# Order of TensorE's work in the first attention layer of a four-layer block, with the pieces of work around its edges

## The chip, the cores and the metric

One Trainium2 chip, one core. The time is that of one execution on the device, in microseconds (us). Five engines run programs of their own and meet at semaphores: TensorE (PE, matrix products), VectorE (DVE), ScalarE (ACT), GpSimdE (POOL) and SyncE (SP, which issues the DMAs here). DMAs move data between HBM and the SBUF; products land in the PSUM's eight banks.

## What is computed

```python
x = x + cross_attn_two_texts(x, ctx)         # layer l0: 20 heads of 8, keys 0..76 "text", 77..511 "ip"
n = layer_norm(x) * g1 + b1;  x = x + attention(n, n)       # layer a1: 20 heads of 64
n = layer_norm(x) * g2 + b2;  x = x + attention(n, ctx)     # layer a2: 20 heads of 64, 512 keys
n = layer_norm(x) * g3 + b3;  x = x + geglu(n @ w1 + b1) @ w2 + b2    # layer ff
```

x is (8, 256, 160), ctx is (8, 512, 256), all float32. In l0, softmax runs over the text keys and the ip keys apart, and the two weighted sums are added. Its projections are q = x Wq, k = text Wk, v = text Wv and the same for ip.

## The kernel before, in words

The eight batches stay in SBUF (`xs`), and the four layers run one after the other, each layer's first steps woven into the last steps of the one before (a seam). Each engine's program is written out by hand, in the order of calls in `build`; no scheduler moves anything, so an instruction that waits holds up all that stand behind it on its engine. Float32 products that must be exact are split into a high and a low part (`hi`, `lo`) in the fp32r type and taken as three products.

**Layer l0** goes in steps t = 0..39 (5 groups of 4 heads for each of 8 batches), a step in four slots s = 0..3. For step t and slot s TensorE's `part(t, s)` (L1689) issues, in this order:
- `score(t, s)` (L1535): scores of group t, into two PSUM banks in turn (`pscore`). For t in 3..34, the middle, a slot with even s issues two of them, s and s + 1, and a slot with odd s none. VectorE's `maximum` (L1867) reduces each to row maxima in two instructions.
- `turned_scores(t-2, s)` (L1550): the same scores with keys on the partitions, into the one bank pair `pst`, which ScalarE's `exp` (L1750) reads; the next one waits for that exponential.
- in slots 0 and 2 half of `weighted_sums(t-3)` (L1638), into `px`.
- in slot 2 `turn_max(t-1)` (L1650): the maxima of the group before are transposed into the bank `pj`; VectorE's `place_max` (L1874) adds them from there to `q4`. On VectorE it is called in slot 2 behind `maximum(t, 2)`.
- in slot 3 of some steps `finish` (L1656, into `px`); then `project(t, s)`, where the plan has something for that slot: a projection of the next batch (L1560, L1567, L1573), the output product (L1662), or a reciprocal's spreading (L1656). All of these but the first values go to `pj`, and each waits until the last user of `pj` has been read.

`EARLY` (L1380) is the plan of the first five steps; `PLAN` that of the others. What is in `FIRST` but not in `EARLY` (`AHEAD`) is projected before step 0.

**The weights of the layers behind** are loaded, copied to `hi` (ACT or POOL) and subtracted to `lo` (POOL) inside the steps of the layer before. For a1 this is `opening(k, s)`, k = t - 24: `WV_HI` (L428) lists the slots in which ACT copies wv's six pieces. The first of them waits for the last stacking DMAs of l0 (`ahead["moved"]`), since it overwrites memory in their reach. POOL rounds each group's stacked keys and queries (`round_stack`, L2005, L2006) and splits each batch's inputs (`split_inputs`, L1971 to L1965).

**Seams.** l0 to a1: for d = 0..2 the four slots of step 40 + d are woven with the two halves of a1's step d. a1 to a2: the context of the first batch is loaded, copied to `hi` by ACT (L1078) and subtracted by POOL (L1281) in a2's `opening(39)`. a2 to ff: VectorE splits w1 and makes the first norm (`xhat`, `n32`) in `opening(k)` behind the last steps of a2.

Of the kernel before, what the change touches and what calls it, by code (L numbers as in the profile page):

```python
# [18 lines left out]
D1 = 64  # L19
INNER = HEADS * D1  # L20
FF = 4 * C
P = 128
# [327 lines left out]
def high_n(act_copy, w, raw_w):  # L350


    act_copy(w[:, 0:2], raw_w[:, 0:2])
    return act_copy(w[:, 4], raw_w[:, 2])


def low_n(subtract, w, raw_w):

    subtract(w[:, 2:4], raw_w[:, 0:2], w[:, 0:2].bitcast(FP32))
    for h in range(2):  # L360
        rows = slice(h * D1 + REST, (h + 1) * D1)
        last = subtract(w[rows, 4], raw_w[rows, 2], w[rows, 4].bitcast(FP32))
    return last


# [16 lines left out]
def self_attention_layer(nc, ctx, places, tag, xs, dram, ln, ahead, next_norm, next_nt):  # L382
# [43 lines left out]


    WV_HI = [(11, 0), (11, 2), (12, 0), (12, 1), (13, 0), (13, 1)]  # L428
# [251 lines left out]
    def vector(dve):  # L680
# [37 lines left out]
        def part(d, i):  # L718
            if here(d - 1):
                if d == 1 and i == 0:  # L720
                    dve.wait_ge(negmax_zeroed, 1)
                maximum(d - 1, i)

        def rest(d):
            if here(d):
                low_queries_keys(d)
# [14 lines left out]
        return dict(opening=opening, part=part, rest=rest)  # L741

    def gpsimd(pool):
# [7 lines left out]
        def opening(k):  # L751
# [36 lines left out]
            if k in (12, 13):  # L788
                pool.wait_ge(wv_hi, 2 * (k - 12) + 2)
                low(wv, k - 12).then_inc(wv_done, 1)  # L790
            if k == 14:
                pool.wait_ge(wv_hi, 6)
                low_rows(wv, wv_done)
                ln.pool_lo(pool, 0, nts[0])
# [17 lines left out]
def cross_attention_layer(nc, ctx, places, tag, xs, dram, ctx_t, ln, nt, ahead, load_next):  # L812
# [42 lines left out]
    ctx_in, c_hi, c_ready = sem("ctx_in"), sem("c_hi"), sem("c_ready")  # L855
# [220 lines left out]
    def scalar(act):  # L1076
# [32 lines left out]
        def opening(d):  # L1109


            if d == 26:
                act.wait_ge(loaded[0], 16)
                high_n(copy, wq, raws["wq"]).then_inc(w_hi, 1)
# [10 lines left out]
            if d == 39:  # L1125
                for s in range(4):
                    high_context(0, s)
# [26 lines left out]
    def vector(dve):  # L1154
        def subtract(out, x, y):
            return nc.vector.tensor_tensor(out, x, y, ALU.subtract)  # L1156

        def low_context(m, s):
            dve.wait_ge(c_hi, 4 * m + s + 1)
# [46 lines left out]
        def opening(d):  # L1206

            if d == 27:
                dve.wait_ge(w_hi, 1)
# [4 lines left out]
            if d == 38:  # L1214
                nc.vector.memset(ones[:], 1.0).then_inc(ones_set, 1)

        def part(d, s):
# [9 lines left out]
            if s == 1 and norm_at(d, LN_STATS):  # L1227
# [7 lines left out]
            if s == 3 and here(d):  # L1235
                low_keys(d)

# [8 lines left out]
    def gpsimd(pool):  # L1246
# [12 lines left out]
        def opening(d):  # L1259
# [6 lines left out]
            if 29 <= d < 33:  # L1266
                s = d - 29
                pool.wait_ge(w_hi, 2)
                nc.gpsimd.tensor_tensor(wk[1][:, s], raws["wk"][:, s], wk[0][:, s].bitcast(FP32),
                                        ALU.subtract).then_inc(wk_done, 1)  # L1270
            if 34 <= d < 38:
                s, cols = (d - 34) // 2, slice((d % 2) * (INNER // 2), (d % 2 + 1) * (INNER // 2))
                pool.wait_ge(w_hi, 3)
# [4 lines left out]
            if d == 39:  # L1278
                for s in range(4):
                    pool.wait_ge(c_hi, s + 1)  # L1280
# [24 lines left out]
def narrow_attention_layer(nc, ctx, places, tag, xs, ident, dram, x_t, ctx_t, load_first, first_in, next_norm):  # L1305
# [67 lines left out]
    def here(g):  # L1373
# [26 lines left out]
    def in_pj(use):  # L1400
        what, m = use
        return not (what[0] == "v" and m < 2)
# [118 lines left out]
    def tensor(pe):  # L1521
# [104 lines left out]
        def weighted_sums(g, half):  # L1626

            m, u = divmod(g, GROUPS)
            if half == 0:
# [3 lines left out]
                if m > 1:  # L1633
# [6 lines left out]
            if half == 1:  # L1640
                last.then_inc(px_ready, 1)

# [46 lines left out]
        def part(t, s):  # L1689


            if here(t) and not V_LAG <= t < ALL - GROUPS:
                score(t, s)
            elif here(t) and s % 2 == 0:
                score(t, s)
                score(t, s + 1)
            if here(t - T_LAG):
                turned_scores(t - T_LAG, s)
            if s in (0, 2) and here(t - V_LAG):
                weighted_sums(t - V_LAG, s // 2)  # L1700
            if s == 2 and here(t - 1):
# [3 lines left out]
            if projected(t, s):  # L1705
                project(*projected(t, s))

# [823 lines left out]
```

## Time and profile before

| | us |
|---|---|
| median of 3 runs | 1583.85 (1581.68 to 1603.56) |
| the profiled execution | 1598.35 |
| its span, first to last instruction | 1596.6 |
| TensorE's mean granted clock in it | 0.968 |
| TensorE busy in it | 1512.6 (95%) |
| VectorE busy | 1082.2 (68%) |
| ScalarE busy | 773.1 (48%) |
| GpSimdE busy | 439.1 (28%) |

The profile is of one execution, 14.5 us above the median. Engine rows give start, duration, engine, line, operation, output and inputs, count; in brackets the idle time before and what ended it. Ends of matmuls are modelled. [...]

### The profile page before, as it was taken

To read this page: it belongs to the slowest core of one execution; us is meant where nothing else is said; L and a number is where in the kernel's file an instruction comes from. 1 tells how busy PE (TensorE), PEld (TensorE's weight loads), DVE (VectorE), ACT (ScalarE), POOL (GpSimd) and SP (SyncE) were. 2 spreads that over 40 slices of the span, in tenths; PEclk is the share of its full clock that TensorE was granted. 3 is DMA by queue.
4 is the path that set the end of the run, shared out by engine and by line. 5 is a ranking of instruction groups with operands and counts; after the bars stand their busy time and mean duration, and the time that the engine had idled before them with its cause. 6 is when DMAs were issued, how large, how long until landed. Compare 5 with 4: busy or idle time off the path is not lost.

```text
span 1596.6 us, 40717 instructions
## 1 busy us (share of the span) xinstructions
PE 1512.6 (95%) x17888; PEld 1190.1 (75%) x17888; DVE 1082.2 (68%) x1515; ACT 773.1 (48%) x1061; POOL 439.1 (28%) x395
## 2 busy tenths in 40 slices
PE   7999999888999999999899999999999999999988
PEld 6556665546888887888678888788888888787788
DVE  5677777662767777767566677676766677676666
ACT  3666666654444455555344444444444454443423
POOL 3333335340222322433321222122211222121300
PEclk7799999977999999999999999999999999999999
DMA  5322222300000020000210010101000020000000
GB/s 153 92 59 59 59 79 69 92 2 2 23 2 2 8 86 2 6 2 4 52 48 2 2 28 1 28 2 28 2 22 7 2 71 2 2 2 1 2 13 21
DMA packets 27211, 45.51 MB, mean 29 GB/s; under 512 B 7392, under 2 KB 15520, under 8 KB 26656
## 3 DMA queue, kind: packets, MB, share of 16 engines
q1 hardware_dynamic: 27040, 42.96, 9.1%
q8 instruction: 140, 2.29, 0.6%
q14 instruction: 31, 0.25, 0.0%
HBM read 29.51 MB, written 1.31 MB: 19 GB/s over the span
## 4 chain that ended last, share of the span: by engine, by line
PE 71%; ACT 8%; DVE 8%; issue 6%; POOL 3%; SPq 2%; DMA 1%; ACTq 0%; POOLq 0%; DVEq 0%
PE a_pj L999 7%; PE a_pj L987 6%; PE a_pj L528 4%; PE a_pv L1021 4%; PE a_px L1021 4%; PE a_px L569 3%; PE l_px L1638 3%; PE a_pv L555 2%; PE a_px L1036 2%; PE l_pst L1550 2%; ACT l_probs L1750 2%; PE a_pscore L931 2%; PE a_pst L952 2%; PE a_px L555 2%; PE a_pj L537 2%
## 5 line engine op out<-in xcount | busy, mean ns | idle before, releaser
L1256 POOL TENSOR_TENSOR a_key_sum<-a_probs 128x512 f32<-128x512 f32 x120 | 159.1, 1330 | 471.7 <-ACT a_probs L1089 471.7
L1168 DVE TENSOR_REDUCE a_negmax<-a_pscore 128x2 f32<-128x1024 f32 x160 | 195.6, 1223 | 106.7 <-PE a_pscore L931 106.3
L1089 ACT ACTIVATE a_probs<-a_pst 128x1024 f32<-128x1024 f32 x160 | 164.0, 1025 | 167.7 <-PE a_pst L958 167.1
L1867 DVE TENSOR_REDUCE l_negmax<-l_pscore 128x2 f32<-128x154 f32 x320 | 201.2, 682 | 55.9 <-PE l_pscore L1535 55.9
L1750 ACT ACTIVATE l_probs<-l_pst 128x1024 f32<-128x1024 f32 x160 | 163.9, 1025 | 90.0 <-PE l_pst L1550 89.7
L748 POOL TENSOR_TENSOR a_key_sum<-a_probs 128x1024 f32<-128x1024 f32 x40 | 96.3, 2407 | 239.0 <-ACT a_probs L617 239.0
L689 DVE TENSOR_REDUCE a_negmax<-a_pscore 128x4 f32<-128x1024 f32 x80 | 97.7, 1221 | 45.9 <-PE a_pscore L486 45.8
L999 PE MATMUL a_pj<-a_wv_hi,a_ct 128*128 128x256 f32 x640 | 112.5, 288 | 0.8
L1193 DVE RECIPROCAL a_recip<-a_pv 128x256 f32<-128x256 f32 x40 | 70.2, 1756 | 45.8 <-PE a_pv L1027 45.8
L617 ACT ACTIVATE a_probs<-a_pst 128x1024 f32<-128x1024 f32 x80 | 81.8, 1023 | 38.9 <-PE a_pst L512 38.1
L1550 PE MATMUL l_pst<-l_q,l_k 32*128 32x256 f32 x640 | 80.2, 330 | 19.7 <-ACT l_probs L1750 19.2
L952 PE MATMUL a_pst<-a_qh,a_kh 64*128 64x256 f32 x640 | 96.1, 293 | 2.7 <-ACT a_probs L1089 1.8
L701 DVE RECIPROCAL a_recip<-a_pv 128x256 f32<-128x256 f32 x40 | 70.3, 1757 | 41.4 <-PE a_pv L560 40.9
L987 PE MATMUL a_pj<-a_ct,a_wk_hi 64*128 64x512 f32 x640 | 94.2, 412 | 2.5 <-POOL a_ct L1281 1.4
L1550 PEld LDWEIGHTS l_pst<-l_q,l_k 32*128 32x128 f32 x640 | 57.2, 202 | 51.4 <-ACT l_probs L1750 43.6
L1638 PE MATMUL l_px<-l_probs,l_v 128*32 128x256 f32 x1280 | 95.2, 419 | 0.0
L954 PE MATMUL a_pst<-a_qh,a_kl 64*128 64x256 f32 x640 | 91.5, 279 | 0.0
L999 PEld LDWEIGHTS a_pj<-a_wv_hi,a_ct 128*128 128x128 f32 x640 | 89.7, 189 | 2.4 <-DVE a_kl L1156 2.3
L958 PE MATMUL a_pst<-a_neg_t,a_sel 64*128 64x256 f32 x640 | 91.1, 277 | 0.0
L956 PE MATMUL a_pst<-a_ql,a_kh 64*128 64x256 f32 x640 | 90.9, 276 | 0.0
L1078 ACT ACTIVATE a_neg_t<-a_pscore 128x256 fp32r<-128x256 f32 x40 | 15.4, 384 | 148.5 <-PE a_pscore L1044 148.5
L1078 ACT ACTIVATE a_v<-a_pj 128x1024 f32<-128x1024 f32 x40 | 41.1, 1027 | 94.0 <-PE a_pj L999 94.0
(239 smaller groups left out, 3654.4 us busy)
## 6 DMA issues: line engine op xcount, KB each, us to landing
l_ct<-in_ctx_t SPq DMA_DIRECT2D x8, 512.0 KB, 3.7
l_k_stack<-l_k_hi SPq DMA_DIRECT2D x64, 64.0 KB, 2.1
a_ct<-in_ctx_t SPq DMA_DIRECT2D x8, 512.0 KB, 4.8
a_ct<-in_ctx_t SPq DMA_DIRECT2D x16, 256.0 KB, 5.6
l_q_stack<-l_q_hi SPq DMA_DIRECT2D x80, 32.0 KB, 1.9
a_raw_wv<-in_a_wv SPq DMA_DIRECT2D x2, 1280.0 KB, 8.4
l_x<-in_x_t SPq DMA_DIRECT2D x8, 256.0 KB, 3.9
l_k_stack<-l_k_lo SPq DMA_DIRECT2D x32, 64.0 KB, 2.1
```

Source lines behind the costliest of these rows:

```text
L689: nc.vector.tensor_reduce(to, pscore[:].rearrange("p h (q k) -> p h q k", q=QT), AX.X, ALU.max, negate=True).then_inc(max_done, 1)
L952: mm(pst[:, h, to], kh[OWN[h], kb, i, kt], qh[OWN[h], qb, i, :], start=True, stop=False)
L987: last = mm(pj[:, t, :], wk[hw][OWN[t], s, u * P:(u + 1) * P], cts[b % 2][OWN[t], hc, s, :], start=k == 0, stop=k == len(C_ROWS) - 1)
L999: last = mm(pj[:, kt // 2, (kt % 2) * STEP_COLS:(kt % 2 + 1) * STEP_COLS], cts[b % 2][:, hc, 2 * s, kt * P:(kt + 1) * P], wv[hw][:, s, u * ...
L1021: mm((pv, px)[x][t * 32:(t + 1) * 32, 0:SQ], v[:, e % 2, kt, t * D1 + x * 32:t * D1 + (x + 1) * 32], probs[:, t, kt, :], start=kt == 0, st ...
L1089: nc.scalar.activation(probs[:, 2 * i:2 * i + 2, 2 * n:2 * n + 2, :], pst[:].rearrange("p h (k q) -> p h k q", k=2), ACT.Exp, scale=SCALE) ...
L1168: nc.vector.tensor_reduce(to, pscore[:], AX.X, ALU.max, negate=True).then_inc(max_done, 1)
L1256: nc.gpsimd.tensor_tensor(key_sums[n][:, two], probs[:, two, 2 * n, :], probs[:, two, 2 * n + 1, :], ALU.add).then_inc(half_summed, 1)
L1550: last = mm(pst[:, h, i * SQ:(i + 1) * SQ], k4[rows, u, kt * P:(kt + 1) * P], q4[rows, u, :], start=True, stop=True)
L1638: last = mm(px[j * ROWS:(j + 1) * ROWS, 0:SQ], vs[m % 2][:, kt, GROUP * u + j, :], probs[g % 2][:, j, kt, :], start=kt == 0, stop=kt == KT ...
L1750: nc.scalar.activation(probs[g % 2][:, 2 * pair:2 * pair + 2, 2 * n:2 * n + 2, :], pst[:].rearrange("p h (k q) -> p h k q", k=2), ACT.Exp, ...
L1867: last = nc.vector.tensor_reduce(to[:, :, k], pscores[s % 2][:, :, keys], AX.X, ALU.max, negate=True)
```

## The change

1. *SBUF addresses* of nearly all tensors (`AT`) are laid out anew.
2. *First steps*: `EARLY` is another plan. The values v1 and v2 of batch 0 are projected ahead of step 0, those of batch 1 come in steps 0, 1, 3 and 4, no longer all in steps 1 and 2.
3. *Middle of l0*: a pair of scores is issued behind the slot's turned scores and weighted sums, no longer ahead of them.
4. *Unread products*: in odd slots of steps 3 to 39 in which nothing is projected or finished, `fill` issues four products of 128x256 that nobody reads.
5. *Weights' pieces*: ACT's six pieces of wv move to later slots; POOL's subtractions for wq and wk are spread over two steps; a2's wq copy is two instructions in two steps.
6. *Seam l0 to a1*: a1's second half step of d = 1 comes ahead of l0's slots 2 and 3 there, and VectorE splits the first queries and keys of a1 between l0's slots 2 and 3.
7. *Seam a1 to a2*: half of the first context is copied and subtracted by VectorE; `maximum` of slot 1 of a2's step 2 comes ahead of a1's normalisation.
8. *Seam a2 to ff*: VectorE's pieces for ff come in slot 1 of their step, with the norm ahead of the split of w1.

```diff
-    WV_HI = [(11, 0), (11, 2), (12, 0), (12, 1), (13, 0), (13, 1)]
+    WV_HI = [(12, 0), (12, 1), (12, 3), (13, 0), (13, 1), (13, 3)]
...
@@ l0, TensorE and the plan
-    EARLY = {(0, 0): ("v1", 0), (0, 1): ("v2", 0), (0, 2): ("ip", 1), (0, 3): ("v3", 0),
-             (1, 0): ("text", 1), (1, 1): ("v0", 1), (1, 2): ("v1", 1), (1, 3): ("v2", 1),
-             (2, 0): ("v3", 1), (2, 1): ("q", 1), (2, 3): ("rest", 1)}
+    EARLY = {(0, 0): ("v3", 0), (0, 1): ("ip", 1), (0, 2): ("v0", 1), (1, 0): ("v1", 1), (1, 1): ("text", 1),
+             (2, 1): ("q", 1), (2, 3): ("rest", 1), (3, 1): ("v2", 1), (4, 1): ("v3", 1)}
...
+        def fill(t, s):
+            if s == 1:
+                pe.wait_ge(pj_read, pj_uses["turn", t - 1])
+            else:
+                pe.wait_ge(px_read, px_uses["sum", t - V_LAG] + 1)
+            k = k4[:, (t - 1) % GROUPS]
+            for _ in range(4):
+                mm((pj if s == 1 else px)[:, 0:SQ], k[:, 0:P], k[:, 0:SQ], start=True, stop=True)
...
-            if here(t) and not V_LAG <= t < ALL - GROUPS:
+            middle = V_LAG <= t < ALL - GROUPS
+            if here(t) and not middle:
                 score(t, s)
-            elif here(t) and s % 2 == 0:
-                score(t, s)
-                score(t, s + 1)
             if here(t - T_LAG):
                 turned_scores(t - T_LAG, s)
             if s in (0, 2) and here(t - V_LAG):
                 weighted_sums(t - V_LAG, s // 2)
+            if middle and s % 2 == 0:
+                score(t, s)
+                score(t, s + 1)
             if s == 2 and here(t - 1):
                 turn_max(t - 1)
             if s == 3 and finished(t):
                 finish(*finished(t))
             if projected(t, s):
                 project(*projected(t, s))
+            elif s % 2 and V_LAG <= t < ALL and not (s == 3 and finished(t)):
+                fill(t, s)
...
@@ a1, POOL's opening
-                if k == first + 2:
+                if k == first + 1:
                     for s in range(2):
                         low(w, s).then_inc(done, 1)
+                if k == first + 2:
+                    pool.wait_ge(*ahead["rounded_in"](OPENED + k))
                     low_rows(w, done)
...
@@ a2, VectorE's opening
+            if d == 39:
+                dve.wait_ge(ctx_in, 48)
+                for s in range(2):
+                    nc.vector.tensor_copy(cts[0][:, 0, s], ct32[:, s]).then_inc(c_first, 1)
+                for s in range(2):
+                    dve.wait_ge(c_first, s + 1)
+                    low_first(s)
...
@@ build, TensorE (ACT the same; DVE with split_first in (0, 1))
             for d in range(3):
                 for i in range(2):
+                    if (d, i) == (1, 1):
+                        own["part"](d, i)
                     first["part"](S0 + d, 2 * i)
+                    if (d, i) == (0, 1):
+                        own["split_first"]()
                     first["part"](S0 + d, 2 * i + 1)
-                    own["part"](d, i)
+                    if (d, i) != (1, 1):
+                        own["part"](d, i)
...
@@ build, VectorE, a1 to a2 and a2 to ff
             cross["part"](2, 0)
+            cross["part"](2, 1)
             own["rest"](S1 + 2)
-            for s in range(1, 4):
+            for s in range(2, 4):
                 cross["part"](2, s)
...
                 for s in range(4):
                     cross["part"](d, s)
+                    if s == 1 and FF_OPEN <= d:
+                        last["opening"](d - FF_OPEN)
                 cross["rest"](d)
-                if FF_OPEN <= d:
-                    last["opening"](d - FF_OPEN)
+                if d == FF_OPEN + 2:
+                    last["scale_first"]()
```

## Rows read from the trace of the kernel before

**Rows 1.** The page: granted clock of TensorE in 40 slices of the span, in tenths

```profile
PEclk7799999977999999999999999999999999999999
```

**Rows 2.** Six stretches of l0: length, busy time of PE, PEld, DVE, ACT, POOL, clock, DMA

```profile
20.50:51.20 30.70, 30.67 (x124) 22.00 (x126) 16.20 (x27) 10.80 (x21) 6.81 (x11) 0.50 0.48 143
80.00:85.00 5.00, 3.96 (x39) 2.14 (x39) 3.94 (x7) 3.55 (x5) 2.17 (x3) 1.00 0.01 2
85.00:90.00 5.00, 5.00 (x32) 3.03 (x30) 1.91 (x4) 2.43 (x3) 0.00 (x0) 0.54 0.06 15
121.60:161.50 39.90, 38.01 (x371) 24.71 (x370) 30.34 (x50) 26.73 (x38) 14.76 (x20) 1.00 0.21 59
269.70:273.10 3.40, 3.40 (x21) 2.01 (x23) 0.87 (x2) 1.40 (x3) 2.75 (x7) 0.50 0.17 42
314.00:337.90 23.90, 19.01 (x116) 10.21 (x116) 9.60 (x16) 13.04 (x18) 4.90 (x7) 0.50 0.02 6
```

**Rows 3.** Timeline of TensorE: slots 2 and 3 of one middle step

```profile
133.95 0.50 PE L1535 MATMUL l_pscore<-l_k,l_q 32*128 32x512 f32 x4
134.31 0.50 PE L1550 MATMUL l_pst<-l_q,l_k 32*128 32x256 f32 x4
134.75 1.07 PE L1638 MATMUL l_px<-l_probs,l_v 128*32 128x256 f32 x16
135.75 0.44 PE L1650 MATMUL l_pj<-identity,l_negmax 128*128 128x128 f32 x2
136.11 0.50 PE L1550 MATMUL l_pst<-l_q,l_k 32*128 32x256 f32 x4
136.70 0.90 PE L1573 MATMUL l_pj<-l_wc,l_ct 128*128 128x160 f32 x6
137.53 0.86 PE L1535 MATMUL l_pscore<-l_k,l_q 32*128 32x512 f32 x4
```

**Rows 4.** Timelines of VectorE and ScalarE in the same two slots

```profile
134.50 1.29 DVE L1867 TENSOR_REDUCE l_negmax<-l_pscore 128x2 f32<-128x154 f32 x2 [0.63 <-PE l_pscore L1535]
136.22 0.42 DVE L1874 TENSOR_TENSOR l_q<-l_q,l_pj 128x256 fp32r<-128x256 f32 x1 [0.44 <-PE l_pj L1650]
...
133.24 1.02 ACT L1750 ACTIVATE l_probs<-l_pst 128x1024 f32<-128x1024 f32 x1 [0.60 <-PE l_pst L1550]
134.86 1.02 ACT L1750 ACTIVATE l_probs<-l_pst 128x1024 f32<-128x1024 f32 x1 [0.38 <-PE l_pst L1550]
```

**Rows 5.** Timeline of TensorE: two starts of steps, five steps apart, and a 256-column projection

```profile
121.58 0.50 PE L1535 MATMUL l_pscore<-l_k,l_q 32*128 32x512 f32 x4
...
155.74 1.24 PE L1560 MATMUL l_pj<-l_nt,l_wq 128*128 128x256 f32 x8
...
161.52 0.50 PE L1535 MATMUL l_pscore<-l_k,l_q 32*128 32x512 f32 x4
```

**Rows 6.** Timeline of TensorE: last work ahead of step 0, its start, start of step 3

```profile
15.54 1.75 PE L1573 MATMUL l_pscore<-l_wc,l_ct 128*128 128x320 f32 x6
18.86 0.50 PE L1535 MATMUL l_pscore<-l_k,l_q 32*128 32x512 f32 x2 [1.56 <-DVE l_q L1942]
...
49.10 0.80 PE L1535 MATMUL l_pscore<-l_k,l_q 32*128 32x512 f32 x4
```

**Rows 7.** Timelines of TensorE and ScalarE: step 35, and the start of step 40

```profile
308.42 0.42 PE L1550 MATMUL l_pst<-l_q,l_k 32*128 32x256 f32 x4
317.77 0.79 PE L1550 MATMUL l_pst<-l_q,l_k 32*128 32x256 f32 x4 [6.24 <-ACT l_probs L1750]
...
362.46 0.79 PE L1550 MATMUL l_pst<-l_q,l_k 32*128 32x256 f32 x4
...
316.07 0.74 ACT L611 ACTIVATE a_wv_hi<-a_raw_wv 128x640 fp32r<-128x640 f32 x1 [6.11 <-DMA l_q_stack<-l_q_lo]
```

**Rows 8.** Timelines: a stall of TensorE in step 30 and one at a seam

```profile
269.07 2.39 PE L1567 MATMUL l_pj<-l_ct,l_wc 128*128 128x512 f32 x6 [1.49 <-POOL l_nt L1965]
...
804.78 0.49 PE L931 MATMUL a_pscore<-a_kh,a_qh 64*128 64x512 f32 x2 [1.92 <-DVE a_negmax L1168]
```

More of the change, by code:

```diff
@@ L40 @@
 AT = {
[24 rows of a table removed]
[19 rows of a table added]
+    210944, "ff_hidden": 5152, "ff_gains": 48672, "a2_ct32": 184160, "ff_ln_half": 48704, "a1_ln_shift": 86336,
[4 rows of a table added]
 }
@@ L347 @@
 STEP_COLS = 2 * P
[L350 to L363, printed above, removed]
 class SplitMatrix:
@@ L425, in self_attention_layer @@
     y_ready, y_taken = sem("y_ready"), sem("y_taken")
-    WV_HI = [(11, 0), (11, 2), (12, 0), (12, 1), (13, 0), (13, 1)]
+    OPENED = ahead["steps"] - 16
+    WV_HI = [(12, 0), (12, 1), (12, 3), (13, 0), (13, 1), (13, 3)]
     WV_HALF = dram["wv"].shape[2] // 2
@@ L722, in part, with split_first @@
                 maximum(d - 1, i)
+        def split_first():
+            low_queries_keys(0)
         def rest(d):
-            if here(d):
+            if here(d) and d > 0:
                 low_queries_keys(d)
@@ L739, in rest @@
                 normalise(d - 3)
-        return dict(opening=opening, part=part, rest=rest)
+        return dict(opening=opening, part=part, rest=rest, split_first=split_first)
     def gpsimd(pool):
@@ L787, in opening @@
                 nc.gpsimd.memset(ones[:], 1.0).then_inc(ones_set, 1)
-            if k in (12, 13):
-                pool.wait_ge(wv_hi, 2 * (k - 12) + 2)
-                low(wv, k - 12).then_inc(wv_done, 1)
+            if k == 12:
+                pool.wait_ge(wv_hi, 2)
+                low(wv, 0).then_inc(wv_done, 1)
+            if k == 13:
+                pool.wait_ge(wv_hi, 4)
+                low(wv, 1).then_inc(wv_done, 1)
+                ln.pool_lo(pool, 0, nts[0])
             if k == 14:
                 pool.wait_ge(wv_hi, 6)
+                pool.wait_ge(ln.n_ready, 1)
                 low_rows(wv, wv_done)
-                ln.pool_lo(pool, 0, nts[0])
         def step(d):
@@ L1113, in opening @@
                 act.wait_ge(loaded[0], 16)
-                high_n(copy, wq, raws["wq"]).then_inc(w_hi, 1)
+                copy(wq[:, 0:2], raws["wq"][:, 0:2]).then_inc(w_hi, 1)
+            if d == 27:
+                copy(wq[:, 4], raws["wq"][:, 2]).then_inc(w_hi, 1)
             if d == 28:
@@ L1125, in opening @@
             if d == 39:
-                for s in range(4):
+                for s in (2, 3):
                     high_context(0, s)
@@ L1156, in subtract, with low_first @@
             return nc.vector.tensor_tensor(out, x, y, ALU.subtract)
+        def low_first(s):
+            subtract(cts[0][:, 1, s], ct32[:, s], cts[0][:, 0, s].bitcast(FP32)).then_inc(c_ready, 1)
         def low_context(m, s):
-            dve.wait_ge(c_hi, 4 * m + s + 1)
+            dve.wait_ge(c_hi, 4 * m + s - 1)
             subtract(cts[m % 2][:, 1, s], ct32[:, s], cts[m % 2][:, 0, s].bitcast(FP32)).then_inc(c_ready, 1)
@@ L1208, in opening @@
             if d == 27:
-                dve.wait_ge(w_hi, 1)
+                dve.wait_ge(w_hi, 2)
                 for h in range(2):
@@ L1226, in part @@
                     ln.dve_lo(dve, norm_at(d, LN_SPLIT), nt)
-            if s == 1 and norm_at(d, LN_STATS):
+            if s == 1 and d > 1 and norm_at(d, LN_STATS):
                 ln.dve_stats(dve, norm_at(d, LN_STATS))
@@ L1236, in part @@
                 low_keys(d)
+            if (d, s) == (1, 3):
+                ln.dve_stats(dve, norm_at(d, LN_STATS))
         def rest(d):
@@ L1267, in opening @@
                 s = d - 29
-                pool.wait_ge(w_hi, 2)
+                pool.wait_ge(w_hi, 3)
                 nc.gpsimd.tensor_tensor(wk[1][:, s], raws["wk"][:, s], wk[0][:, s].bitcast(FP32),
@@ L1278, in opening @@
             if d == 39:
-                for s in range(4):
-                    pool.wait_ge(c_hi, s + 1)
+                for s in (2, 3):
+                    pool.wait_ge(c_hi, s - 1)
                     nc.gpsimd.tensor_tensor(cts[0][:, 1, s], ct32[:, s], cts[0][:, 0, s].bitcast(FP32),
@@ L1401, in in_pj @@
         what, m = use
-        return not (what[0] == "v" and m < 2)
+        return not (what == "v3" and m == 0 or what in ("v0", "v1") and m == 1)
     def finished(t):
@@ L1632, in weighted_sums @@
                     pe.wait_ge(first_read, 4)
-                if m > 1:
+                if m > 0:
                     pe.wait_ge(pj_read, pj_uses["v3", m] + 1)
@@ L2165, in opening @@
             if k == 1:
+                dve.wait_ge(small_in, 64)
+                ln.dve_xhat(dve, 0)
+            if k == 2:
                 dve.wait_ge(w_hi, 1)
@@ L2168, in opening @@
                                         ALU.subtract).then_inc(w_done, 1)
-                dve.wait_ge(small_in, 64)
-                ln.dve_xhat(dve, 0)
-            if k == 2:
+            if k == 3:
                 dve.wait_ge(w_hi, 2)
@@ L2180, in opening, with scale_first @@
                 ln.dve_xhat(dve, 1)
+        def scale_first():
+            ln.dve_n32(dve, 0)
         def batch(b):
@@ L2197, in batch @@
                                     ALU.add).then_inc(y_taken, 1)
-        return dict(opening=opening, batch=batch)
+        return dict(opening=opening, scale_first=scale_first, batch=batch)
     def gpsimd(pool):
@@ L2334, in _ @@
                 for i in range(2):
+                    if (d, i) == (1, 1):
+                        own["part"](d, i)
                     first["part"](S0 + d, 2 * i)
                     first["part"](S0 + d, 2 * i + 1)
-                    own["part"](d, i)
+                    if (d, i) != (1, 1):
+                        own["part"](d, i)
                 own["rest"](d)
@@ L2371, in _ @@
                 for i in range(2):
+                    if (d, i) == (1, 1):
+                        own["part"](d, i)
                     first["part"](S0 + d, 2 * i)
+                    if (d, i) == (0, 1):
+                        own["split_first"]()
                     first["part"](S0 + d, 2 * i + 1)
-                    own["part"](d, i)
+                    if (d, i) != (1, 1):
+                        own["part"](d, i)
                 own["rest"](d)
```

7 lines of the change are left out of this document (3 added, 4 removed), and 47 rows, old and new, of the table AT.

## The prediction

> **What bounds the kernel now.** I read the page's slices first. TensorE's clock falls short of full in the first two slices and again in slices 9 and 10, which are l0's start and its end [rows 1]. Then I took stretches of l0. In the middle TensorE is busy for 38.01 of 39.90 us at full clock; in 20.5 to 51.2 it is busy all the time, at half clock [rows 2]. So a step of the middle can lose little idle time, while the edges hold idle time and half-clock time. The timelines tell which wait ends last at each place.
>
> One middle step shows the structure [rows 3, 4]. Turned scores of two slots can't follow each other in less than about 1.62 us: the exponentials start at 133.24 and 134.86, and each takes 1.02 and a hand-over each way. Slot 2 goes: scores 133.95, turned scores 134.31, weighted sums 134.75, turned maxima 135.75, next turned scores 136.11, projection 136.70. VectorE starts its maximum 0.55 us behind the scores (134.50), finishes it, waits 0.44 for the transposed maxima and places them at 136.22. The projection at 136.70 starts 0.48 us behind that: it writes `pj`, which `place_max` reads. This hand-over, not TensorE's own work, already sets that start.
>
> **The middle of l0 (part 3).** Durations by starts: turned scores 0.33 to 0.43, weighted sums 1.00, scores 0.36, transposes 0.36. In slots 0 and 1 the move is a small gain: the scores fill time in which the next turned scores wait for the exponential, and slot 1 is shorter by 0.34 where it is longer than 1.62. In slots 2 and 3 it is a loss. From the slot's turned scores on, the scores now start at about 1.33 us instead of 0.36 before them. VectorE's maximum starts at 1.33 + 0.55 = 1.88 and ends 1.29 later, at 3.17. `place_max` is called behind it and the projection starts 0.48 behind `place_max`: 3.65. Before, it was 136.70 - 134.31 = 2.39. The projection of slot 3 is late by 1.26 us, and behind it on TensorE stand the next step's turned scores and everything else. TensorE had 0.15 us to spare there; now it stands idle for about 1.2 us.
>
> VectorE can't help itself: `place_max` stands behind a maximum whose scores come late. [...]
>
> The five kinds of step, from [rows 3 to 5] and the plan: slots 2 and 3 take 3.65 us plus the projection (0.8 to 1.7 us), so the five together take about 23.7 us instead of 19.9; slots 0 and 1 take about 19.3 instead of 20.04, after ACT's copies of the last projection, which now stand ahead of the first exponential, have taken back half of the gain. That is +3.8 - 0.8 = +3.0 us on the 39.94 between the two starts of [rows 5]. Five such rounds (t = 10 to 34) give **+15**. Bounds: if the wait is hidden, the 0.34 saved per odd slot remains, -7.5; if the delay of slot 1 adds to it, +20.
>
> **First steps (part 2).** TensorE idles for 1.56 us ahead of step 0 [rows 6]; v1 and v2 fit into that. Steps 0 to 2 take 49.10 - 18.86 = 30.2 us, at half clock, with TensorE dense. The new plan takes four of eleven products out of them (v1, v2 of batch 0 to the front, v2, v3 of batch 1 to steps 3 and 4). Such a product takes 0.83 at full clock (136.70 to 137.53, [rows 3]), up to twice that at half, say 1.5 us: -6, of which VectorE's pace may give 1.5 back, so at least -4.5. [...] I take **-12**, bounds -4.5 and -14. Steps 3 to 9 lose 0.5 to 1 in the ordinary steps and gain where a half-clock stretch such as that from 85 on [rows 2] goes: **-2** (-5 to +2).
>
> **Unread products (part 4).** Eight slots: (3,3), (4,3), (7,1), (36,1), (37,3), (38,1), (38,3), (39,1). A 256-column product takes 1.24 / 8 = 0.15 us, four 0.6, all eight slots 4.9 us if exposed. They stand in slots that wait for the exponential, so I cost them at nothing; without that cover, +4.9. Their worth is the clock, and it is in the terms here.
>
> **Weights' pieces (part 5).** ACT's first piece of wv waits 6.11 us for a stacking DMA in step 35, and the exponential behind it holds TensorE for 6.24; then 23.9 us pass at half clock [rows 7, 2]. One step later (the new slot) is 7 us later, past the DMA's landing at 316. From 308.42 to the start of step 40 at 362.46 are 54.0 us for five steps; at full clock and without the stall they take about 7.1 each (four slots of 1.62 make 6.5, and slot 2 is longer) and 2 more for one output product, 37.5. I take **-14**, bounds -6 (the stall alone) and -17. The POOL pieces were late into step 30 and stalled the projection 1.49 us [rows 8], and 3.4 us at half clock follow it [rows 2]; POOL's wide subtractions now come a step sooner, while it waits for stacking DMAs: **-3**, bounds 0 and -3.5.
>
> **Seams (parts 6 to 8).** TensorE waits 1.92 us for a maximum at 804.78, the pattern of four such stalls of 1.6 to 1.9 us for VectorE [rows 8]: one at the seam to a1, this one, and two at the seam to ff. Each gets the work it waits for moved ahead. With one more wait at the first seam, and with the clock's falls next to the first two: **-4, -4 and -3**. VectorE's share of the first context puts some 2.2 us in front of a maximum of a1, which costs TensorE about what it saves it. Bounds of the three together: 0 and -14. Addresses (part 1): nothing.
>
> **The clock in the middle.** An idle 1.15 us in three of five steps may let the clock fall. [...] I allow two falls at 3 us: **+6**, bounds 0 and +25.
>
> **The sum**, against the profiled execution: 1598.35 - 12 - 2 + 15 - 14 - 3 - 4 - 4 - 3 + 6 = 1577.4. The median stands 14.5 below that execution, and half-clock stretches that come and go are the likely reason; the change takes most of these away in any run, so little of the 14.5 is to be had twice. I take 3.4 off for it: **1574**.
>
> **The rivals.**
> - *The clock falls often in the middle.* One fall in every fourth of 32 steps, at 3 us, is +24, in place of the +6: 1592; one in every second step is +48: 1616. From about five falls on the change is no gain over 1583.85. For it: the stretch at 80 to 85. [...] 0.20, at 1594.
> - *The middle costs nothing.* Place and projection find cover that I don't see, and the exponentials' earlier start counts: -15 from the sum, and no falls (-6), 1553 to 1560. Against it: the projection's start hangs on `place_max` already now [rows 3, 4]. 0.13, at 1557.
> - *The edges give less*, since undisturbed runs do not have the half clock that the profile shows: the start -5 and the last steps -7 instead of -12 and -14, so +14: 1588. For it: the 14.5 us between median and profile. 0.17.
> - *My forecast*: 0.50, own range 1564 to 1584.
>
> **How the numbers follow.** 1574 is the forecast. Up to 0.2 may be left out: the range goes from 1556 to 1600. Within 2% is 1552.2 to 1615.5, about what a measurement of this kernel can tell from no change. Faster needs the second rival at its far end: 0.05. Slower needs a fall in every second step: 0.05. The same: 0.90.
>
> **What would show it.** The step's row of `l_pj` in slot 3 should carry an idle time of 1.0 to 1.3 us put down to VectorE's L1874, in steps without `finish`, and five steps of the middle should take 43 us instead of 39.94. No wait for `l_q_stack` should stand before `a_wv_hi`, and step 3 should start near 37. If five steps take 38 to 40 us, the middle is wrong; if the middle's clock isn't 1.00, the first rival holds. I am wrong in sign if the middle costs over 25 us.

## The result, and the profile after

| | before | after |
|---|---|---|
| median of 20 runs each, us | 1592.66 (1580.38 to 1603.56) | 1598.84 (1593.11 to 1603.13) |
| span of the profiled execution, us | 1596.6 | 1595.5 |
| TensorE's mean granted clock in it (1.00 is full clock, 0.50 half) | 0.968 | 0.979 |

The ratio after to before is 1.0045, 95% interval 1.0023 to 1.0067: the change costs 0.4%, surely more than nothing and well within 2%. The forecast was 1574, the range 1556 to 1600: the result lies just inside the range, 24.8 us above the forecast, and on the other side of the kernel before (a gain of 10 us was forecast, against 1583.85). The three runs of before that the forecast knew (1583.85) lay low; over twenty, before stands 8.8 us higher, and its profiled execution only 5.7 above the median.

The page of the kernel after, granted clock in 40 slices. The low slices of [rows 1] at 9 and 10 are gone; slices 5 and 7, in the middle of l0, are a little lower than before:

```profile
PEclk8999898999999999999999999999999999999899
```

Stretches of l0 in the kernel after, in the columns of [rows 2]. They are: a half-clock stretch in the first steps; five steps of the middle; two half-clock stretches in the middle; the last steps.

```profile
27.10:40.80 13.70, 13.08 (x49) 8.29 (x51) 9.17 (x16) 5.67 (x9) 4.38 (x6) 0.50 0.54 155
120.90:164.22 43.32, 39.04 (x371) 24.38 (x370) 30.27 (x50) 26.71 (x38) 14.79 (x20) 1.00 0.20 55
177.20:190.80 13.60, 13.23 (x83) 7.21 (x84) 7.57 (x11) 5.88 (x8) 6.68 (x9) 0.50 0.22 55
269.20:286.20 17.00, 16.63 (x98) 9.43 (x88) 9.65 (x15) 6.67 (x8) 7.79 (x12) 0.50 0.17 43
323.40:369.50 46.10, 44.33 (x437) 27.52 (x433) 34.68 (x56) 33.00 (x43) 18.47 (x15) 1.00 0.05 12
```

Five steps take 43.32 us at full clock with the same 371 records of TensorE as the 39.90 us of [rows 2]; the engine is busy for 39.04 of them and was for 38.01. The first steps have less than half of the half-clock time of [rows 2] (13.7 us of 30.7), and the last ones none.

Timelines of the kernel after, TensorE and then VectorE, in slots 2 and 3 of one middle step (they answer [rows 3, 4]; here the turned scores are L1558, scores L1543, weighted sums L1646, turned maxima L1670, `maximum` L1891, `place_max` L1898):

```profile
128.99 0.50 PE L1558 MATMUL l_pst<-l_q,l_k 32*128 32x256 f32 x4 [0.29 <-ACT l_probs L1774]
129.42 1.07 PE L1646 MATMUL l_px<-l_probs,l_v 128*32 128x256 f32 x16
130.42 0.51 PE L1543 MATMUL l_pscore<-l_k,l_q 32*128 32x512 f32 x4
130.86 0.44 PE L1670 MATMUL l_pj<-identity,l_negmax 128*128 128x128 f32 x2
131.22 0.51 PE L1558 MATMUL l_pst<-l_q,l_k 32*128 32x256 f32 x4
132.62 0.90 PE L1581 MATMUL l_pj<-l_wc,l_ct 128*128 128x160 f32 x6 [0.89 <-DVE l_q L1898]
...
130.95 1.29 DVE L1891 TENSOR_REDUCE l_negmax<-l_pscore 128x2 f32<-128x154 f32 x2 [0.80 <-PE l_pscore L1543]
132.16 0.41 DVE L1898 TENSOR_TENSOR l_q<-l_q,l_pj 128x256 fp32r<-128x256 f32 x1
132.49 1.29 DVE L1891 TENSOR_REDUCE l_negmax<-l_pscore 128x2 f32<-128x154 f32 x2
```

The chain is the forecast's: scores 1.43 us behind the slot's turned scores, the maximum 0.53 behind them, `place_max` 1.21 later, the projection 0.46 later, 3.63 us in all, where [rows 3] had 2.39. The turned maxima stood ready since 131.3; VectorE comes to them at 132.16 because its maximum is in front.

The other end of the kernel, the seam a2 to ff. TensorE, VectorE and GpSimdE in the kernel after:

```profile
1496.06 0.80 PE L925 MATMUL a_pscore<-a_kh,a_qh 64*128 64x512 f32 x2 [6.28 <-DVE a_negmax L1167]
...
1492.88 0.36 DVE L167 TENSOR_SCALAR ff_ln_xhat<-xs,ff_ln_mv,ff_ln_rstd 128x160 f32<-128x160 f32 x1 [5.60 <-POOL ff_ln_rstd L160]
...
1494.78 1.22 DVE L1167 TENSOR_REDUCE a_negmax<-a_pscore 128x2 f32<-128x1024 f32 x1
...
1486.33 1.29 POOL L1264 TENSOR_TENSOR a_key_sum<-a_probs 128x512 f32<-128x512 f32 x1 [11.20 <-ACT a_probs L1083]
1488.60 1.28 POOL L1264 TENSOR_TENSOR a_key_sum<-a_probs 128x512 f32<-128x512 f32 x1 [0.98 <-ACT a_probs L1083]
1490.92 1.26 POOL L1264 TENSOR_TENSOR a_key_sum<-a_probs 128x512 f32<-128x512 f32 x1 [1.05 <-ACT a_probs L1083]
1492.14 0.70 POOL L160 TENSOR_TENSOR ff_ln_rstd<-ff_ln_var,ff_ln_half 128x2 f32<-128x2 f32 x1
```

VectorE's second normalisation for ff (L167) now stands in slot 1, and the `rstd` that it reads stands on GpSimdE behind three key sums of the same step, each of which waits for one of ScalarE's exponentials. VectorE waits 5.60 us; the maximum behind it comes late, and TensorE stands for 6.28. In the kernel before, the normalisation came behind the whole step (at 1507.74, without a wait), and `rstd` was there since 1501.9.

**Where the time went.** The two traces cut at the same points of the program: `g` is the group whose maxima are turned, `a` a count of the reciprocals in a1 and a2. (`g4`: the maxima of group 4 are turned, in step 5; the seam a1 to a2 is a37 to a40; ff is taken from VectorE's first `ff_hidden` to its last, and some 5 us of either span lie behind it.) With the old order and no fall of the clock, `both_undone` has 37.1 us from g4 to g9 and `mid_undone` 191.9 from g9 to g33.

| stretch | before | after | difference | forecast |
|---|---|---|---|---|
| start to g4 | 71.3 | 61.2 | -10.1 | -12 |
| g4 to g9 (steps 5 to 10) | 39.7 | 42.5 | +2.8 | -2 |
| g9 to g33 | 195.1 | 219.6 | +24.5 | +15 +6 -3 |
| g33 to g39 | 64.5 | 46.1 | -18.4 | -14 |
| g39 to a1's first | 46.3 | 41.6 | -4.6 | -4 |
| seam a1 to a2 | 42.6 | 38.6 | -4.0 | -4 |
| the rest of a1 and a2 | 1030.0 | 1030.9 | +0.9 | 0 |
| last steps of a2 (a77 to ff) | 39.0 | 46.9 | +7.8 | -3 |
| ff | 62.9 | 62.9 | 0 | 0 |
| sum | | | -1.1 | -21 |

### The profile page after: what moved, and what is told of

It reads as the page before. It is cut to its first block, busy times and chain, and to the rows that moved or that the text cites. A ratio compares the mean times of both kernels' runs of the same rounds, so it can differ in the third digit from the quotient of the medians.

```text
span 1595.5 us, 40782 instructions
## 1 busy us (share of the span) xinstructions
PE 1511.8 (95%) x17920; PEld 1183.7 (74%) x17920; DVE 1085.4 (68%) x1519; ACT 772.1 (48%) x1059; POOL 439.9 (28%) x393
## 4 chain that ended last, share of the span: by engine, by line
PE 74%; DVE 10%; ACT 7%; issue 6%; POOL 2%; DMA 1%; SPq 0%; POOLq 0%; ACTq 0%; DVEq 0%
PE a_pj L993 7%; PE a_pj L981 5%; PE l_px L1646 5%; PE a_pj L514 4%; PE a_pv L1015 4%; PE a_px L1015 4%; PE l_pst L1558 3%; PE a_px L555 3%; DVE l_negmax L1891 3%; PE l_pscore L1543 3%; PE a_px L1030 2%; PE a_pv L541 2%; PE a_pscore L925 2%; PE a_pst L946 2%; PE a_px L541 2%
## 5 line engine op out<-in xcount | busy, mean ns | idle before, releaser
L1891 DVE TENSOR_REDUCE l_negmax<-l_pscore 128x2 f32<-128x154 f32 x320 | 202.6, 686 | 95.2 <-PE l_pscore L1543 94.4
L1646 PE MATMUL l_px<-l_probs,l_v 128*32 128x256 f32 x1280 | 91.3, 405 | 2.5 <-DVE l_ot L1911 2.5
L1558 PE MATMUL l_pst<-l_q,l_k 32*128 32x256 f32 x640 | 80.6, 330 | 8.3 <-ACT l_probs L1774 7.8
L1072 ACT ACTIVATE a_v<-a_pj 128x1024 f32<-128x1024 f32 x40 | 41.1, 1027 | 94.2 <-PE a_pj L993 94.2
L1015 PE MATMUL a_pv<-a_probs,a_v 128*32 128x256 f32 x1280 | 85.5, 385 | 0.0
```

The costliest lines, as they stand in the source:

```text
L1015: mm((pv, px)[x][t * 32:(t + 1) * 32, 0:SQ], v[:, e % 2, kt, t * D1 + x * 32:t * D1 + (x + 1) * 32], probs[:, t, kt, :], start=kt == 0, st ...
L1558: last = mm(pst[:, h, i * SQ:(i + 1) * SQ], k4[rows, u, kt * P:(kt + 1) * P], q4[rows, u, :], start=True, stop=True)
L1646: last = mm(px[j * ROWS:(j + 1) * ROWS, 0:SQ], vs[m % 2][:, kt, GROUP * u + j, :], probs[g % 2][:, j, kt, :], start=kt == 0, stop=kt == KT ...
L1891: last = nc.vector.tensor_reduce(to[:, :, k], pscores[s % 2][:, :, keys], AX.X, ALU.max, negate=True)
```

## The experiments

All times are medians; the ratio is to the kernel before, run beside it on the same chip, with its 95% interval. Seven of the variants have only four runs, so differences of medians and of ratios can part by several us; where they do, both are given. "From" names the kernel that was edited.

| run | from | us | ratio |
|---|---|---|---|
| `mid_alone` | before | 1634.71 | 1.0302 (1.0238 to 1.0367) |
| `mid_undone` | after | 1564.51 | 0.9839 (0.9781 to 0.9898) |
| `place_first` | after | 1575.83 | 0.9903 (0.9871 to 0.9935) |
| `norm_back` | after | 1594.52 | 1.0005 (0.9975 to 1.0035) |
| `both_undone` | mid_undone, norm_back | 1556.41 | 0.9744 (0.9667 to 0.9820) |
| `rstd_first` | mid_undone | 1558.31 | 0.9758 (0.9679 to 0.9837) |
| `take_first` | place_first, norm_back | 1560.37 | 0.9767 (0.9690 to 0.9844) |
| `no_fill` | mid_undone | 1567.97 | 0.9799 (0.9722 to 0.9877) |
| `old_first` | mid_undone | 1573.68 | 0.9853 (0.9776 to 0.9929) |
| `old_wv` | mid_undone | 1579.77 | 0.9931 (0.9902 to 0.9961) |
| `wv_alone` | before | 1580.32 | 0.9918 (0.9874 to 0.9962) |
| `fill_wait` | norm_back | 1576.40 | 0.9893 (0.9829 to 0.9958) |

**1. The order of the middle alone, and everything but it.** `mid_alone` puts it into the kernel before, `mid_undone` takes it out of the kernel after:

```diff
-            middle = V_LAG <= t < ALL - GROUPS
-            if here(t) and not middle:
+            if here(t) and not V_LAG <= t < ALL - GROUPS:
                 score(t, s)
+            elif here(t) and s % 2 == 0:
+                score(t, s)
+                score(t, s + 1)
...
-            if middle and s % 2 == 0:
-                score(t, s)
-                score(t, s + 1)
```

> The kernel before with the order of the middle alone: each pair of scores behind the slot's turned scores and weighted sums (t = 3 to 34). Theory V, the late scores make VectorE place the transposed maxima late and the projection of slot 3 waits for that: slower than before by 17 to 27 us (about 0.65 us in each of 32 steps and up to two falls of the clock), five middle steps take 43.3 us as in the changed kernel, and the idle time ahead of slot 3's projection is 0.9 us, put down to place_max. Rival, the cost of the middle in the changed kernel comes from what stands beside it there (the other plan, the addresses): within 5 us of before.

> The changed kernel with the order of the middle as before. Theory V: the changed kernel stands 6 us above before, and 20 to 27 us go with the middle, so 14 to 21 us faster than before, five middle steps back at 39.9 us. Rival (the middle's cost is not its order): about 6 us slower than before, as the changed kernel.

The order costs 34 us in the kernel after (1598.84 - 1564.51; 33 by the ratios). In the kernel before its price is rough: the five runs of `mid_alone` lie between 1612.19 and 1644.67, 42 us by the median of all five and 32 by that of the three quickest; 17 to 27 were expected. The order is the whole loss and more: without it the change is a gain of 1.6%. The profiled execution of `mid_alone` was the quickest of its five, so its trace does not show some 22 us of the 42. Its mean granted clock is 0.969, that of the other four 0.947 to 0.962, so they spent more time at half clock; at which steps isn't shown. The stretch g9 to g33, columns as in [rows 2], in `mid_alone`:

```profile
115.30:327.80 212.50, 192.21 (x1786) 119.62 (x1782) 146.31 (x247) 130.54 (x189) 84.46 (x107) 0.98 0.23 66
```

and in `mid_undone`:

```profile
100.10:292.00 191.90, 182.84 (x1786) 119.20 (x1783) 147.13 (x248) 130.16 (x188) 84.36 (x107) 1.00 0.26 76
```

TensorE's idle time in the stretch is 9.1 us in `mid_undone` and 20.3 in `mid_alone`.

**2. Whose wait it is.** `place_first` leaves TensorE's program as the change has it and calls VectorE's `place_max(t-1)` ahead of `maximum(t, 2)` in the middle:

```diff
         def part(t, s):
+            ahead_of_max = s == 2 and V_LAG <= t < ALL - GROUPS
+            if ahead_of_max:
+                place_max(t - 1)
             if here(t):
                 maximum(t, s)
...
-            if s == 2 and here(t - 1):
+            if s == 2 and here(t - 1) and not ahead_of_max:
                 place_max(t - 1)
```

> The changed kernel, with VectorE's place_max(t - 1) called ahead of maximum(t, 2) in the middle; TensorE's order is that of the change. Theory V says it is VectorE's order alone that makes the late scores dear: slot 3's projection no longer waits for a maximum, five steps take 38 to 40 us, and the kernel is 14 to 30 us faster than before. Rival, the scores behind the sums are late for something else too (the maxima themselves, the next step's transposes): five steps stay above 41.5 us and the kernel stays within 6 us of before.

23 us of the 34 (1598.84 - 1575.83) come back from a move of one instruction a step on VectorE. Five steps take 41.6 us (43.3 in the kernel after), where 38 to 40 was expected: the total came out as the theory had it, but a part of the wait was left. In the trace of `place_first` the turned maxima start at 127.49 (0.44 long), `place_max` starts at 127.97, the maximum behind it at 128.31 and the projection at 128.45, 0.59 us behind the turned scores of its slot (127.86) where the kernel after has 1.40. In both traces VectorE did the two in the order of its program. The waits of TensorE from g9 to g33 by what ended them (total, times, longest) in the kernel after:

```profile
PE l_pj L1581 <- DVE l_q L1898: 9.1, 10, 0.9
PE l_pst L1558 <- ACT l_probs L1774: 3.4, 13, 0.3
PE l_pj L1676 <- DVE l_q L1898: 2.5, 4, 0.9
PE l_px L1646 <- DVE l_ot L1911: 2.5, 5, 0.5
PE l_pj L1575 <- DVE l_q L1898: 1.4, 5, 0.3
```

and in `place_first`:

```profile
PE l_px L1646 <- DVE l_ot L1911: 6.8, 10, 1.0
PE l_pst L1558 <- ACT l_probs L1774: 4.1, 15, 0.3
```

The wait for the placed maxima (`l_q`) is gone, and one of the same kind has grown: `px` is written again while VectorE's taking of the finished output (`l_ot`) still stands behind a maximum. `take_first` moves that one too, and puts ff's norm back:

```diff
+            take_first = s == 3 and finished(t) and V_LAG <= t < ALL - GROUPS
+            if take_first:
+                take(*finished(t))
             if here(t):
                 maximum(t, s)
```

> place_first with norm_back, and VectorE takes the finished product of slot 3 ahead of maximum(t, 3). TensorE keeps the scores behind the sums. If the rest of the middle's cost is this second hand-over (theory V2: TensorE waits 0.98 and 0.35 us for l_ot in two of five steps), five steps take 40.0 to 40.6 us instead of 41.6, and the kernel takes 1575.8 - 8 - 7 = 1561. Rival, the scores' place costs something that no order on VectorE gives back: five steps stay at 41.3 or more, 1567 or more.

g9 to g33 now takes 195.0 us (five steps 40.5, as expected) and no wait for VectorE is left among TensorE's waits there. With VectorE's program fitted to it, the new order of TensorE's work costs 4.0 us against `both_undone`, run beside it (1560.37 to 1556.41); it gains nothing either.

**3. How much is the wait, how much the clock.** `fill_wait` is `norm_back` with four of the unread products in slot 3 ahead of the projection, in the 20 steps of 5 to 34 without `finish`. It adds 80 products and takes no wait away:

```diff
             if s == 3 and finished(t):
                 finish(*finished(t))
+            if s == 3 and GROUPS <= t < ALL - GROUPS and not finished(t):
+                fill(t, s)
```

> norm_back (the changed kernel with ff's second normalisation behind its step; 1594.5), with four unread products of 128x256 more in slot 3 of the middle steps t = 5 to 34 that finish nothing, ahead of the projection that waits 0.9 us for place_max: 0.6 us of work nobody reads inside idle time. Theory F2 (the wait itself costs 16 to 20 us and the clock's falls that it brings the rest of the 34): five steps stay at 43.3 us, the middle has no stretch at half clock, and the kernel is 5 to 15 us faster than norm_back, near 1585. Rival, the falls have another origin: within 4 us of norm_back, with half-clock stretches in the middle.

18 us less than `norm_back` (1576.40 to 1594.52), from more work; 5 to 15 were expected. It holds in every run: the mean granted clock is 0.991 to 0.993 in the four of `fill_wait`, 0.969 to 0.982 in the ten of `norm_back`. g9 to g33 in `norm_back`:

```profile
106.10:326.90 220.80, 202.19 (x1787) 124.60 (x1783) 146.89 (x247) 130.64 (x189) 84.24 (x107) 0.92 0.23 67
```

In `fill_wait`, slot 3 of a middle step in TensorE's timeline, then g9 to g33 and five steps of it by the columns of [rows 2]:

```profile
129.41 0.50 PE L1558 MATMUL l_pst<-l_q,l_k 32*128 32x256 f32 x4
129.84 0.74 PE L1661 MATMUL l_px<-l_k 128*128 128x256 f32 x4
130.82 0.46 PE L1581 MATMUL l_pj<-l_wc,l_ct 128*128 128x160 f32 x2 [0.23 <-DVE l_q L1900]
...
101.90:310.10 208.20, 197.03 (x1843) 125.02 (x1839) 146.90 (x247) 130.35 (x189) 84.52 (x107) 1.00 0.24 71
...
145.20:188.50 43.30, 41.01 (x386) 25.98 (x382) 30.28 (x50) 26.70 (x39) 14.79 (x20) 1.00 0.20 55
```

The projection starts as late as in the kernel after (1.41 us behind the turned scores, 1.40 there), and five steps still take 43.3 us: the wait is all there. But its idle part shrank from 0.89 to 0.23, and the clock stays at 1.00 through all 208 us. Whether that comes from the shorter idle time or the added products, this run can't tell. The three traces separate the two prices, from g4 to g33: 229.0 us with the old order and no fall (37.1 + 191.9), 249.3 in `fill_wait`, 262.1 in the kernel after. The wait costs 20.3 us, the falls 12.8.

**4. The norm at the last seam.** `norm_back` puts ff's second `xhat` behind its step again; `both_undone` does so in `mid_undone`; `rstd_first` keeps it in slot 1 and calls GpSimdE's `rstd` ahead of that step's key sums:

```diff
@@ norm_back, VectorE
-            if k == 5:
-                ln.dve_xhat(dve, 1)
...
+                if d == FF_OPEN + 5:
+                    last["second_xhat"]()
@@ rstd_first, GpSimdE
+                if d == FF_OPEN + 5:
+                    last["opening"](d - FF_OPEN)
                 cross["step"](d)
-                if FF_OPEN <= d:
+                if FF_OPEN <= d and d != FF_OPEN + 5:
```

> The changed kernel, with VectorE's normalisation of ff's second batch (opening(5)) again behind the step and not in its slot 1. Theory N: in slot 1 it waits for rstd, which stands on GpSimdE behind the key sums of that step, so a maximum comes 6 us late, and the clock falls after it: without that the kernel is 7 to 12 us faster than the changed kernel, so 1 to 6 us faster than before. Rival, the fall of the clock at 1489 would come anyway and the wait is hidden at another place: still about 6 us slower than before, with a wait of the same size elsewhere in the last steps of a2.

> The changed kernel with the middle's order of before and with ff's second normalisation behind its step: the two edits that cost time undone. If the costs add up (theory A), it is 7 to 9 us below mid_undone (1564.5), so near 1556 and 33 to 40 us faster than before. Rival, the two touch (the clock falls elsewhere instead): within 3 us of mid_undone.

> mid_undone, with GpSimdE's rstd of ff's second batch called ahead of the key sums of that step; VectorE's normalisation stays in slot 1. Theory N (the wait is for GpSimdE's order alone): the wait of 5.6 us and TensorE's 6.3 us behind it go, and the time is that of both_undone within 3 us, near 1556. Rival, the normalisation in slot 1 is too much for VectorE whatever it waits for: above 1561.

The step from one reciprocal of a2 to the next (a77 to a78) takes 23.6 us after, 15.8 before, 15.7 in `norm_back` and `both_undone`, 18.2 in `rstd_first`. By the medians the norm is worth 4.3 us (`norm_back` against after, 6 by the ratios, where 7 to 12 were expected) and 8.1 (`both_undone` against `mid_undone`, run on another chip; 15 by the ratios). The step's own 7.9 us lie between. `norm_back`'s trace had a half-clock stretch of 41.0 us in the last steps of l0 that the kernel after's did not have. In `rstd_first` `rstd` is early, and the work itself still stands in front of the maximum. TensorE, VectorE and GpSimdE there:

```profile
1458.30 0.79 PE L925 MATMUL a_pscore<-a_kh,a_qh 64*128 64x512 f32 x2 [1.86 <-DVE a_negmax L1167]
...
1453.85 0.53 DVE L167 TENSOR_SCALAR ff_ln_xhat<-xs,ff_ln_mv,ff_ln_rstd 128x160 f32<-128x160 f32 x1
...
1457.03 1.22 DVE L1167 TENSOR_REDUCE a_negmax<-a_pscore 128x2 f32<-128x1024 f32 x1
...
1441.74 0.70 POOL L160 TENSOR_TENSOR ff_ln_rstd<-ff_ln_var,ff_ln_half 128x2 f32<-128x2 f32 x1
```

So both halves are shown: the wait for GpSimdE's `rstd` (6.28 us of TensorE's time, and 10.2 us at half clock that begin inside that wait, at 1491.3) and the normalisation's 3.2 us of VectorE in front of a maximum (1.86). `both_undone` beats both kernels: 1556.41.

**5. The parts that gain.** `old_first` puts the old `EARLY` into `mid_undone` (with the bank waits that go with it), `old_wv` the old slots of wv's pieces; `wv_alone` puts the new slots into the kernel before; `no_fill` takes the unread products out of `mid_undone`:

```diff
@@ old_first
-    EARLY = {(0, 0): ("v3", 0), (0, 1): ("ip", 1), (0, 2): ("v0", 1), (1, 0): ("v1", 1), (1, 1): ("text", 1),
-             (2, 1): ("q", 1), (2, 3): ("rest", 1), (3, 1): ("v2", 1), (4, 1): ("v3", 1)}
+    EARLY = {(0, 0): ("v1", 0), (0, 1): ("v2", 0), (0, 2): ("ip", 1), (0, 3): ("v3", 0),
+             (1, 0): ("text", 1), (1, 1): ("v0", 1), (1, 2): ("v1", 1), (1, 3): ("v2", 1),
+             (2, 0): ("v3", 1), (2, 1): ("q", 1), (2, 3): ("rest", 1)}
@@ old_wv (wv_alone the reverse, in the kernel before)
-    WV_HI = [(12, 0), (12, 1), (12, 3), (13, 0), (13, 1), (13, 3)]
+    WV_HI = [(11, 0), (11, 2), (12, 0), (12, 1), (13, 0), (13, 1)]
@@ no_fill
-            elif s % 2 and V_LAG <= t < ALL and not (s == 3 and finished(t)):
-                fill(t, s)
```

> mid_undone with the plan of the first five steps as before (and the bank rules that go with it). My reading of the traces puts 8 to 10 us on the new plan (step 4's transposes 71.3 before, 60.3 in mid_undone): 6 to 11 us slower than mid_undone, with the clock low for 20 us and more from step 0 on. Rival, the start's gain comes from the unread products and from luck with the clock: within 3 us of mid_undone.

> mid_undone with the six pieces of wv in the slots of before. Theory W (the first piece waits for the stacking DMA and holds the exponential): TensorE stalls 5 to 7 us in step 35 again and the clock falls behind it: 10 to 18 us slower than mid_undone. Rival, the DMA is there in time by now since GpSimdE's pieces are spread: within 3 us.

> The kernel before with the wv pieces in the slots of the change, and nothing else. Theory W: 8 to 16 us faster than before, the time from the start of step 35 to that of step 40 falls from 54 us to below 46. Rival, in runs that are not the profiled one the clock recovers sooner and only the stall of 6 us goes: 4 to 7 us faster.

> mid_undone without the eight slots of unread products, 32 products in all, which nobody reads. If they hold the clock up (theory F), it falls more often in steps 3 to 9 and 36 to 41, and the kernel is 4 to 15 us slower than mid_undone (1564.5). Rival 1, they do nothing: within 3 us. Rival 2, they cost their own 4.9 us: 3 to 5 us faster.

The wv slots are worth 15.3 us in the one kernel and 12.3 in the other (1592.66 - 1580.32). `old_wv` brings the stall of [rows 7] back (5.82 us), and a half-clock stretch of 10.1 us that begins inside it. TensorE, ScalarE, and that stretch:

```profile
306.50 0.79 PE L1558 MATMUL l_pst<-l_q,l_k 32*128 32x256 f32 x4 [5.82 <-ACT l_probs L1773]
...
304.80 0.74 ACT L597 ACTIVATE a_wv_hi<-a_raw_wv 128x640 fp32r<-128x640 f32 x1 [5.69 <-DMA l_q_stack<-l_q_lo]
...
303.20:313.30 10.10, 6.80 (x36) 3.86 (x36) 2.04 (x4) 5.59 (x8) 1.48 (x4) 0.50 0.04 9
```

In the traces g33 to g39 is 54.1 us in `old_wv` and 45.3 in `mid_undone`: 8.8 of the 12.7 us by which these two executions differ. The first steps are worth 9.2 us by the medians, 2 by the ratios, and start to g4 is 68.5 us in `old_first` against 60.0 to 63.5 in the kernels with the new plan and the old middle. But the other two kernels with the old plan took only 62.8 (`wv_alone`) and 64.4 (`mid_alone`): they had 13.6 us at half clock up to there, as the kernel after had (13.7), where `old_first` had 27.3 and the kernel before 37.5. At this equal half clock the old plan is 1.6 and 3.2 us behind the kernel after; whether the new plan prevents the longer half clock isn't shown. The unread products are worth 3.5 us by the medians, and by the ratios the kernel without them is the quicker one (0.9799 against 0.9839): their gain isn't shown. Put into a wait that TensorE really has, as in `fill_wait`, 80 more of them came with 18 us less.

## Why the prediction was wrong, point by point

The sum was 1577.4 against an execution of 1598.35, and the profiled execution after took 1597.29. The 19.9 us between lie in these terms (differences between the two traces, by the table):

- *First steps, -12*: measured -10.1. The half clock shrank from 30.7 us to 13.7, and step 3 starts at 40.57, where 37 was forecast and [rows 6] had 49.10. The size was 2 us too good, and no run shows the 12 as such: the recorded arithmetic carries -4.5 to -6 of it. That the new plan is what took the half clock away isn't shown: two traces with the old plan took 62.8 and 64.4 us to g4, near the 61.2 here.
- *Steps 3 to 9, -2*: measured +2.8. A failed step: these steps have the middle's new order too. The five of them cost 4.0 us of wait in `fill_wait` against `both_undone` (41.1 to 37.1), and a fall of 3.4 us 1.4 more. The prediction allowed 0.5 to 1 us for the order there and charged its full price only from step 10 on. The half clock that it hoped to see go (6.8 us, from 85.4) went.
- *The middle, +15*: right as far as it went. 3.63 us of chain against 3.65, 43.32 us for five steps against 43, an idle time of 0.89 to 0.91 against 1.0 to 1.3, on the line named. (The scores start 1.43 us behind the turned scores, not 1.33; [rows 3] has 0.44 + 1.00 for it. `place_max` comes 1.21 behind the maximum's start, not 1.29, and the two errors cancel.) From g9 to g33 the wait costs 16.3 us (208.2 - 191.9).
- *The clock in the middle, +6*: mis-sized, at 12.8 from g4 on, 11.4 of it from g9 on. The number of falls was right, two large ones (and one of 3.4 us ahead of them), but not their size: 13.7 and 17.1 us long, they cost 5.0 and 6.5 us (the five steps that hold them take 48.3 and 49.8 us, not 43.3), and the three together 12.8. The prediction's 3 us a fall was an allowance that no run shows; the fall of 3.4 us cost 1.4. Its first rival (falls often, 0.20, at 1594) stands nearest to the measured time, but by luck: it has eight short falls for 24 us, and the middle had half of that. Its sign for this rival, a middle clock that isn't 1.00, can't tell it from the forecast, which has two falls itself; the clock was 0.93.
- *Weights' pieces, -14 and -3*: measured -18.4 and -3.0 (the five steps with the stall of [rows 8] took 42.9 us before and 39.9 in `mid_undone`). The edge's bound of -17 was a little too tight: the whole half clock went, and no wait for `l_q_stack` stands before `a_wv_hi`. (`old_wv` puts 8.8 us of this stretch on the slots, `wv_alone` 14.1.)
- *Seams, -4 and -4*: -4.6 and -4.0. The second is the sum of a larger gain and a stall that was too small in the sum: 2.2 us in front of a maximum were said to cost about what they save. VectorE's share of the first context stands for 3.0 us there, and TensorE waits 3.94 us for the maximum; the wait of [rows 8] at this seam is gone. TensorE and VectorE in the kernel after:

```profile
762.75 0.80 PE L472 MATMUL a_pscore<-a_qkh 64*128 64x256 f32 x4 [3.94 <-DVE a_negmax L675]
...
758.53 0.76 DVE L1218 CAST a_ct<-a_ct 128x512 fp32r<-128x512 f32 x2 [0.43 <-DMA a_ct<-in_ctx_t]
759.20 2.36 DVE L1152 TENSOR_TENSOR a_ct<-a_ct 128x512 fp32r<-128x512 f32 x2
761.48 1.21 DVE L675 TENSOR_REDUCE a_negmax<-a_pscore 128x4 f32<-128x1024 f32 x1
```

- *Seam to ff, -3*: the step that failed outright, +7.8. The prediction saw stalls for VectorE there and took the move ahead for their cure. It did not ask what the moved `xhat` itself waits for. Its `rstd` comes from GpSimdE, whose order the change left as it was. The stalls it meant to cure (1.62 and 1.63 us) shrank to 0.92 and 1.09.
- *From the execution to the median*: 3.4 us were taken off, on the ground that before's profile stood 14.5 above its median. Over twenty runs it stood 5.7 above, and after's stood 1.5 below. These 7.2 us are why the medians part by +6.2 where the profiled executions part by -1.1. The base, too, stood 8.8 us lower in the three runs than in twenty, which says nothing of the change.

Steps 5 to 9 (4.8 us), the norm (10.8) and the falls from g9 on (5.4) are more than the whole of the 19.9 us; the first steps (1.9), the wait itself (1.3) and a1 and a2 (0.9) add to it, and the last steps of l0 gave 4.4 back. The sign condition, "wrong if the middle costs over 25 us", was met: it costs 27.7 from g9 on and 33.1 from g4 on.

## What to carry to other kernels

When an instruction moves on one engine, follow two lists: what it reads and when the other engines' programs, in their unchanged order, deliver that; and what stands behind it. A reordering of TensorE's work should be tried together with the order of VectorE's answers to it: one instruction a step moved there took back 23 of 34 us. And a wait that came in most steps had a second loss beside it here: 12.8 us in half-clock stretches, next to 20.3 for the wait itself. With work that nobody reads in the idle part of the wait, there were no such stretches and the 12.8 us were gone.

## What the runs showed of the hardware

With idle times of 0.9 us, three in five steps, and TensorE busy for 39.04 of 43.32 us, the middle had two stretches of 13.7 and 17.1 us at half clock (0.50); with 0.23 us in their place and 41.01 of 43.30 us busy there was none in 208 us. The falls came at other places and in other numbers from trace to trace: at 177 and 269 us in the kernel after, at 180 and 228 in `norm_back`, and in `mid_alone`, with the same 43.3 us for five steps, only one of 3.4 us came between 113 and 320. In the half-clock stretches of the middle TensorE is busy nearly all the time (13.23 of 13.60 us, 16.63 of 17.00), so its waits vanish from the rows just where the time is lost: the slices of the clock show it, the list of waits does not.
